# The ninth tap's product summed by VectorE and joined in TensorE, GpSimd left with 14 adds an image, and a new order of the first stage

## What is computed

```
x = x + deformable(norm_over_channels(x))          # 8 groups, 9 taps, BN, SiLU
t = tokens(x)
t = t + experts0(norm_over_channels(t))            # top 2 of 8
x = image(t)
x = x + attention(norm_over_channels(x))           # 8 heads of 32
t = tokens(x)
t = t + experts1(norm_over_channels(t))            # top 2 of 16
# deformable: y = 1x1(x); v = 1x1(y); offsets and mask from a depthwise 3x3 of y
# out[p] = sum over taps k of mask[p,k] * bilinear(v, p + tap k + offset[p,k])
# z = SiLU(BN(1x1(1x1(out))))
```

## Time and profile before

| | |
|---|---|
| profiled execution | 949.5 us, span 947.7 us |
| median of three runs | 950.69 us |
| mean granted TensorE clock | 0.734 |
| busy: PE, DVE, ACT, POOL | 606.0, 559.3, 318.0, 465.9 us |
| GpSimd's adds (L1344) | 128, 301.0 us |
| first stage | 0 to about 480 us |

### The profile page before, as it was taken

How to read it: one execution, slowest core, us unless ns; L and a number is a source line. 1 busy time by engine, 2 the same in 40 slices (tenths; PEclk the granted TensorE clock), 3 DMA queues, 4 the chain that set the end, 5 groups by cost and what they waited for, 6 DMA issues and landing times.

```text
span 947.7 us, 10354 instructions
## 1 busy us (share of the span) xinstructions
PE 606.0 (64%) x3032; PEld 447.6 (47%) x3032; DVE 559.3 (59%) x1034; ACT 318.0 (34%) x520; POOL 465.9 (49%) x364
## 2 busy tenths in 40 slices
PE   1676868677777768664238888883677772566601
PEld 0445556455655556543126566562566552444400
DVE  3257587887859686986335656653646664434411
ACT  2435352615134423400025555452313230333400
POOL 0058768889888789898510000002557644000075
PEclk9858686758577757755559999997877785667655
DMA  9363534554645453520045445440000000445311
GB/s 360 126 149 80 130 86 117 164 139 136 151 136 142 130 148 75 136 67 0 22 148 163 157 145 180 146 134 14 14 21 30 26 20 22 117 135 136 101 33 36
DMA packets 67014, 101.23 MB, mean 107 GB/s; under 512 B 25742, under 2 KB 45198, under 8 KB 66958
## 3 DMA queue, kind: packets, MB, share of 16 engines
q1 hardware_dynamic: 62416, 93.07, 34.3%
q0 software_dynamic: 4096, 6.30, 2.3%
q10 hardware_dynamic: 446, 1.20, 0.4%
HBM read 37.67 MB, written 25.10 MB: 66 GB/s over the span
## 4 chain that ended last, share of the span: by engine, by line
POOL 25%; PE 24%; issue 21%; DVE 11%; ACT 9%; SPq 6%; DMA 4%; POOLq 0%; DVEq 0%; ACTq 0%
POOL sb_acc L1344 12%; POOL sb_yg L1375 5%; POOL xs L1356 5%; PE ps_pa L475 3%; PE ps_t L510 3%; PE ps_c L468 2%; PE ps_t L577 2%; PE ps_pb L595 2%; DVE sb_hats L1153 2%; DVE sb_prod L1076 2%; ACT sb_hats L850 2%; POOL sb_rs L1383 1%; PE ps_t L578 1%; SPq L406 1%; SPq L405 1%
## 5 line engine op out<-in xcount | busy, mean ns | idle before, releaser
L1344 POOL TENSOR_TENSOR sb_acc<-sb_acc,sb_prod 128x1024 f32<-128x1024 f32 x128 | 301.0, 2377 | 36.3 <-DVE sb_prod L1076 35.6
L1375 POOL DMA_INDIRECT sb_yg<-ys,sb_jdx x64 | 61.6, 962 | 293.6 <-DMA ys<-sb_yt 275.5
L510 PE MATMUL ps_t<-sb_vbd,sb_hx 128*128 128x256 f32 x576 | 143.6, 396 | 76.9 <-DVE sb_prod L1076 71.5
L1076 DVE TENSOR_TENSOR sb_prod<-ps_t,sb_hy 128x1024 f32<-128x1024 f32 x128 | 153.8, 1215 | 61.0 <-PE ps_t L510 49.0
L510 PEld LDWEIGHTS ps_t<-sb_vbd,sb_hx 128*128 128x128 f32 x576 | 112.2, 272 | 109.0 <-DVE sb_prod L1076 73.9
L1356 POOL DMA_INDIRECT xs<-sb_xr,sb_idx x64 | 63.4, 991 | 23.9 <-issue 15.1
L1206 DVE TENSOR_TENSOR sb_hid<-ps_t,sb_hid 114x512 f32<-114x512 f32 x69 | 46.4, 686 | 44.2 <-ACT sb_hid L871 40.6
L496 PE MATMUL ps_c<-sb_dwT,sb_omx 128*128 128x256 f32 x144 | 55.8, 545 | 15.0 <-DVE sb_hats L1062 11.6
L871 ACT ACTIVATE sb_hid<-ps_t 114x512 f32<-114x512 f32 x69 | 41.2, 599 | 46.0 <-PE ps_t L578 46.0
L496 PEld LDWEIGHTS ps_c<-sb_dwT,sb_omx 128*128 128x128 f32 x144 | 37.0, 274 | 25.0 <-issue 18.7
L577 PE MATMUL ps_t<-sb_hx,sb_hats 128*114 128x256 f32 x138 | 42.2, 327 | 0.0
(11 more groups left out here) (253 smaller groups left out, 1295.9 us busy)
## 6 DMA issues: line engine op xcount, KB each, us to landing
sb_hx<-sb_hats SPq DMA_DIRECT2D x384, 96.0 KB, 2.2
xs<-sb_x3t SPq DMA_DIRECT2D x32, 512.0 KB, 5.4
sb_acc<-in_wcat SPq DMA_DIRECT2D x16, 876.0 KB, 4.4
sb_yrep<-in_wcat SPq DMA_DIRECT2D x7, 876.0 KB, 4.4
sb_nt<-xs SPq DMA_DIRECT2D x32, 128.0 KB, 2.1
sb_acc<-in_ucat SPq DMA_DIRECT2D x22, 160.0 KB, 2.4
sb_xt<-xs SPq DMA_DIRECT2D x23, 128.0 KB, 2.1
ys<-sb_yt SPq DMA_DIRECT2D x16, 128.0 KB, 2.5
```

Source lines behind the costliest of these rows:

```text
L510: last = mm(tb[u % 2][:, j * 256:(j + 1) * 256], hx[q % 3][:, j, o:o + P], vbd[n % 2][:, j * 256:(j + 1) * 256], start=True, stop=True)
L1076: v.tensor_tensor(o.rearrange("p (g c q) -> p g c q", g=G, q=H), tb[u % 2][:, :].rearrange("p (g c q) -> p g c q", g=G, q=H), w, ALU.mult) ...
L1344: g.tensor_tensor(acc[n % 2][:, t, :], acc[n % 2][:, t, :], prod[a % 3][:, :], ALU.add).then_inc(s_pool_acc, 1)
L1375: g.indirect_dma_start(out=yg[b][:, t, z, :], out_offset=None, in_=ys[0:NJT[m] * TILE, :], in_offset=bass.IndirectOffsetOnAxis(ap=jdx[m][: ...
```

## The change

- GpSimd no longer adds the ninth tap's two products (`ADDS` is 14 an image). VectorE sums each of them over rows from its `prod` buffer, right behind the product, into `dlast`. A buffer is free when the add of three before is done; for the ninth tap's that is the image's last add.
- TensorE's `sampled` turn is no longer two transposes: for each half it multiplies `dsum` and `dlast` by the identity into the same PSUM place, so that their sum comes out turned.
- ScalarE writes SiLU back into PSUM; `zT` goes. VectorE's `x1` reads it there. Statistics and scaling of the first routing read the tokens from the PSUM bank `pb` instead of `x1t`, which ScalarE still writes.
- The cast of the slot numbers moves from VectorE to ScalarE, as a step `slots`, in both routings.
- The order of the first stage is new on all five engines. Behind it only ScalarE's order gains the second routing's `slots`.

```diff
-ADDS = UNITS - TT
+ADDS = UNITS - 2 * TT
...
 # TensorE, sampled
                 pe.wait_ge(s_dve_dr, n + 1)
+                pe.wait_ge(s_dve_last, n + 1)
...
-                to_channels(pb, dsum).then_inc(s_pe_dt, 1)
+                for t in range(TT):
+                    mm(pb[0:C, t * P:(t + 1) * P], dsum[:, t, :], ident[:, :], start=True, stop=False)
+                    last = mm(pb[0:C, t * P:(t + 1) * P], dlast[:, t, :], ident[:, :], start=False, stop=True)
+                last.then_inc(s_pe_dt, 1)
...
 # ScalarE, z and slots
-                af(zT[:, :], pb[0:C, 0:PIX], ACT.Silu, scale=bns[:, 2:3], bias=bns[:, 3:4]).then_inc(s_act_z, 1)
+                af(pb[0:C, 0:PIX], pb[0:C, 0:PIX], ACT.Silu, scale=bns[:, 2:3], bias=bns[:, 3:4]).then_inc(s_act_z, 1)
...
+            def slots(n, m):
+                act.wait_ge(s_dve_rn[m], n + 1)
+                at = slice(TT * n, TT * n + TT)
+                af(idx[m][:, at, :], slot[m][:, at, :], ACT.Copy).then_inc(s_act_ix[m], 1)
...
 # VectorE, source of stats and norm, tap, x1, slots
-                return (x1t[:, TT * n:TT * n + TT, :], x2t[n % 2], x3t[:, TT * n:TT * n + TT, :])[j - 1]
+                return (tokens(pb), x2t[n % 2], x3t[:, TT * n:TT * n + TT, :])[j - 1]
...
+            def added(a):
+                n, i = divmod(a, UNITS - TT)
+                return ADDS * n + min(i + 1, ADDS)
...
-                a = ADDS * n + (k - 1) * TT + t
+                a = (UNITS - TT) * n + (k - 1) * TT + t
...
-                        dve.wait_ge(s_pool_acc, a - 2)
+                        dve.wait_ge(s_pool_acc, added(a - 3))
...
+                if k == K - 1:
+                    dve.wait_ge(s_dve_p, u + 1)
+                    if n:
+                        dve.wait_ge(s_pe_dt, n)
+                    last = v.tensor_reduce(dlast[:, t, :], o.rearrange("p (c r) -> p c r", r=H), AX, ALU.add)
+                    if t == TT - 1:
+                        last.then_inc(s_dve_last, 1)
...
-                v.tensor_tensor(x1T[:, :], xT[n % 3][:, :], zT[:, :], ALU.add).then_inc(s_dve_x1, 1)
+                v.tensor_tensor(x1T[:, :], xT[n % 3][:, :], pb[0:C, 0:PIX], ALU.add).then_inc(s_dve_x1, 1)
...
-                dve.wait_ge(s_dve_rn[m], 2 * n + 1)
-                v.tensor_copy(idx[m][:, at, :], slot[m][:, at, :]).then_inc(s_dve_rn[m], 1)
...
 # GpSimd, tap and scatter
-                if k == 0:
+                if k in (0, K - 1):
...
-                g.tensor_tensor(acc[n % 2][:, t, :], acc[n % 2][:, t, :], prod[a % 3][:, :], ALU.add).then_inc(s_pool_acc, 1)
+                g.tensor_tensor(acc[n % 2][:, t, :], acc[n % 2][:, t, :], prod[(a + TT * n) % 3][:, :], ALU.add).then_inc(s_pool_acc, 1)
...
-                pool.wait_ge(s_dve_rn[m], 2 * n + 2)
+                pool.wait_ge(s_act_ix[m], n + 1)
```

## The result

| | before | after |
|---|---|---|
| median | 950.16 us (four runs) | 926.19 us (four runs, 925.8 to 928.0) |
| span of the profiled execution | 947.7 us | 924.0 us |
| mean granted TensorE clock | 0.734 | 0.746 |
| busy: PE, DVE, ACT, POOL | 606.0, 559.3, 318.0, 465.9 us | 603.5, 567.6, 321.8, 429.7 us |

The ratio is 0.975 (95% interval 0.9728 to 0.9772): 24 us faster, where some 19 were forecast. The first late scatter stands 24.0 us earlier (430.24 instead of 454.27) and the end of the program 23.7, so the whole gain lies in the first stage.

A forecast was written before the change was run, and what follows sets the result against it. The first stage was taken as bound by VectorE's work plus the holes TensorE's order leaves. Image 0, the periods and the tail summed to 435.3 us against 454.3, −19 us: 932 us forecast, range 916 to 947.

The forecast's parts named there:

- tail: From image 7's first product to the last scatters: 40.1 us instead of 47.3, with 14 GpSimd adds.
- The period of 49.5: Each of images 1 to 4: 40 us of VectorE's work plus 9.3 us of holes left by TensorE.
- the first: Hole at the input product: it and a transpose stand between tap products, VectorE idle 1.5 us.
- the second: Hole at the depthwise convolution, x1 transpose and next tap product: VectorE idle 4.4 us.
- the third: Hole before top-k, during offsets, three value rows, a transpose and logits: VectorE idle 3.4 us.
- The freed steps: Index cast moved to ScalarE, norm's scaling and x1 add reading PSUM: VectorE saves 2.3 us an image.
- The cover at `dsum`: At `dsum`, VectorE's ninth-tap products and reductions, 4.7 us, cover its wait for GpSimd's last two adds, also 4.7.
- What was put at nothing: Side effects costed at zero, among them TensorE's larger sampled turn (about 0.5 us), ScalarE's cast and SiLU in PSUM.
- GpSimd as the bound (917): Rival: GpSimd stays the first stage's bound, gaining 37.6 us less image 0's 4.7; 917 us, chance 0.14.
- The small gain (946): Rival: VectorE's periods stay at 51.9 us, only image 6 and the tail gain; about 946 us, chance 0.08.
- The slower one (957): Rival: late scaling holds TensorE amid value rows, though forecast ready 0.7 us ahead; 957 at 5 us late, chance 0.08.
- That reductions are stretched: Rival: GpSimd stretches VectorE's new reductions like the cast, costing VectorE 20 us more; no chance given.

The follow-up runs named there:

- e4_reduction_twice: Kernel after the change with each of the ninth tap's 16 VectorE reductions made twice: 941.74 us.
- e6_row_twice: Kernel after the change with the first of the depthwise convolution's three rows computed twice on TensorE: 936.91 us.
- e5_twelve_adds: Kernel after the change with the eighth tap's two GpSimd adds left out too, 12 an image, that product summed by nobody: 928.38 us.
- e1_sixteen_adds: Kernel after the change with the ninth tap's adds back on GpSimd, without VectorE's own reductions and TensorE's two extra products: 949.08 us.
- e3_freed_back: Kernel after the change with the index cast back on VectorE and SBUF operands for statistics, scaling and x1 add: 959.59 us.

## Why the prediction came out as it did

**The bound** was named rightly: no engine alone, but VectorE's work plus the holes that TensorE's order leaves. Runs `e4_reduction_twice` and `e6_row_twice` show both terms counting in full, `e5_twelve_adds` that nothing is gained by fewer than 14 adds of GpSimd.

**The sum** was −19 against −24.0. By its terms, forecast and measured: start of image 1 104.2 and 102.7; images 1 to 4 198 and 195.05; image 5 46.5 and 47.4; image 6 46.5 and 44.3; tail 40.1 and 40.8. Image 0 paid less than its 4.7 us because its reductions lie partly where it waited for taps before.

**The period of 49.5** is near the 48.8 measured by two errors against each other. VectorE's work was put at 40 and is 41.3: I carried over the old means of the one-hot and of the block values, but the new order puts both beside GpSimd's adds. The holes were put at 9.3 and are 7.0: the first is right in images 2 to 4 (1.4 to 1.5); the second has 0.7, 3.3, 4.35 and 3.1 us instead of 4.4, as the depthwise product took 2.80 to 4.98 us where I took 4.8; the third is 2.1 instead of 3.4, with logits of 0.61 us where I took 1.0.

**The freed steps**, −2.3 us an image, are the term that failed, though their rows came out as forecast. I priced them at what they took in the old order and added them up. Their worth depends on the order: 5 us (with 16 adds) and 10 us (with 14) in the old, 25 and 33 us in the new. I had the mechanism, but as a rival that I judged apart from them, by the old longest wait of 3.1 us, while it is the PSUM operand that keeps it away. Even so the scaling comes 0.64 us late in images 2 to 4, where my walk had it 0.7 ahead.

**The cover at `dsum`** was right: the ninth tap's products and reductions hide GpSimd's last adds. In `e1_sixteen_adds`, without it, `dsum` waits 3.4 to 3.6 us in each of images 1 to 4; the 23 us that this run loses hold the other waits and the longer tail as well.

**What was put at nothing** nearly was: SiLU takes 0.53 us into PSUM instead of 0.56 into SBUF, the cast 0.21 us on ScalarE. TensorE's sampled turn grew by more than the 0.5 us that I gave it: from 0.63 us at most to 1.96 for image 1 (at 148.21 us), and not where TensorE waits for the norm. VectorE's wait for the tap behind it is 0.3 to 0.5 us in images 2 to 4, and 0.2 in `e1_sixteen_adds`, which has the two transposes.

**The rivals.** GpSimd as the bound (917) falls by `e5_twelve_adds`. The small gain (946) fell with the periods. The slower one (957) is real without the PSUM operands (`e3_freed_back`, 959.6). That reductions are stretched is excluded: 1.22 us, all alike.

The Trainium skill's rule that a PSUM operand caps a step below its double rate (VectorE: DVE Perf Modes, Why PSUM operands drop a tier) speaks against the change; here the scaling takes 0.40 us from PSUM against 0.33 at its shortest from SBUF. The trace agrees in direction, at a price of 0.07 us; against the 1.84 of `e3_freed_back` it saves 1.44.

## What to carry to other kernels

Price a step in the place where the new order puts it, beside what then runs there, and not by its mean in the old one. Parts of a change that meet in one queue don't add: take each away from the whole, and not only add each to the old kernel. An engine that is relieved gains nothing by itself; look for the turn at which others wait for it, and for the cover that the relief brings.

## What the runs showed of the hardware

**The stretch moves from step to step.** A scaling with its operand in SBUF took 0.71 us on average in the old order and 1.84 in the new (60 to 420 us), the one-hot 1.16 and 2.04; in `e3_freed_back` the one-hot was back at 0.60, since GpSimd had run out of adds by then (in the period shown above its adds paused at 234.4 us and the one-hot began at 236.4). Reductions and products from PSUM stayed at 1.21 to 1.22 throughout. The Trainium skill says (SBUF — State Buffer, Who interferes with whom) that on VectorE an instruction with two SBUF inputs contends with GpSimd's reads, that a scaling can contend when it uses both ports, and that on trn2 a reduction never does. These rows agree: the one-hot is of the first kind, the scaling of the second.

**Periods of one order differ with TensorE's clock.** In the kernel after, image 1 took 47.1 us at a granted clock of 0.79 and image 3 took 50.4 at 0.70 (windows above); their steps are the same, but image 1's one-hot was also 1.6 us shorter. The 12 depthwise matmuls of images 2 and 4:

```profile
110.11 2.80 PE L475 MATMUL ps_pa<-sb_ypad,sb_diag 128*64 128x256 f32 x12 [0.20 <-ACT sb_yrep L781]
...
208.15 4.98 PE L475 MATMUL ps_pa<-sb_ypad,sb_diag 128*64 128x256 f32 x12
```

The first ran at a granted clock of 1.00, the upper level (2.4 GHz), the second at 0.55, mostly the lower (1.2 GHz); images 3, 5 and 6 had 0.70, 0.75 and 0.54. Before either, TensorE had computed taps with short pauses, and the clock was already at that level (1.00 and 0.50); what decides which level a piece meets is left open here. The statistics' wait behind the depthwise product is 0.71 us in the first case and 4.35 in the second.
